# Splitting expert weights inside the feed-forward stage and parking them in DRAM, with smaller first batch and a limit on row transfers

## The reference

```python
# layer 0: attention with 16 heads, one k/v head and a computed position bias, then a spiking network
c = layernorm(attention(x))                       # 16 heads of 64
y = square(relu(c @ Wfc.T)) @ Wproj.T             # 256 -> 1024 -> 256
for 5 steps: mem = 0.9*mem + y - (mem > 1); count += (mem_new > 1)
x = x + count / 5
# layer 1: attention with a bias from a side input, then a transformer block with experts
X = layernorm(attention(x, fside))
X = X + mha(rmsnorm(X, g1))                       # 4 heads, one k/v head
xf = rmsnorm(X, g2)
top2 of xf @ Wr.T + bias, softmax weights         # 8 experts
moe = shared(xf) + sum over top2 of weight * expert(xf)   # each: silu(x W1) * (x W3) @ W2, 256 wide
x = x + X + moe
```

## Time and profile before

| | |
|---|---|
| median of 3 runs | 1442.61 us (1438.27 to 1443.07) |
| the profiled execution | 1443.43 us, its span 1441.7 us |
| PE busy | 1307.1 us (91%) |
| DVE busy | 1037.4 us (72%) |
| ACT busy | 897.6 us (62%) |
| POOL busy | 708.2 us (49%) |

### The profile page before, as it was taken

The page is one execution under the profiler, slowest core; times in us unless marked ns, Lnnn a source line. Parts: engine busy times, 40 slices in busy tenths (PEclk is TensorE's granted clock), DMA queues, the critical chain, the costliest instruction groups (busy, mean ns, idle before and its releaser), DMA issues.

```text
span 1441.7 us, 42824 instructions
## 1 busy us (share of the span) xinstructions
PE 1307.1 (91%) x15311; PEld 1157.7 (80%) x15312; DVE 1037.4 (72%) x2148; ACT 897.6 (62%) x2309; POOL 708.2 (49%) x797
## 2 busy tenths in 40 slices
PE   4899999999689999889999999689999789999980
PEld 3799999998579999778888888668788678888870
DVE  4798988988736465687887887768987686555446
ACT  3677777777356666656666666478775354555545
POOL 2556555564435454545445444357777562333330
PEclk8899999999799999999999999899997999999995
DMA  8200000001030000000000000020012623333319
GB/s 230 54 8 10 8 9 9 8 11 37 3 87 1 1 0 1 3 9 10 8 9 9 9 9 12 23 56 16 16 29 72 211 80 111 105 104 101 101 44 349
DMA packets 87025, 71.19 MB, mean 49 GB/s; under 512 B 49981, under 2 KB 80831, under 8 KB 85824
## 3 DMA queue, kind: packets, MB, share of 16 engines
q1 hardware_dynamic: 80320, 51.73, 12.7%
q0 software_dynamic: 6528, 17.05, 3.3%
HBM read 39.47 MB, written 24.02 MB: 44 GB/s over the span
## 4 chain that ended last, share of the span: by engine, by line
PE 56%; issue 20%; POOL 10%; DVE 9%; ACT 3%; DMA 1%; another core or an unknown queue 0%; ACTq 0%; POOLq 0%; DVEq 0%; SPq 0%
PE psQ L2348 9%; PE psQ L1957 7%; PE psW L2035 7%; PE psW L2327 5%; POOL pn L759 5%; PE psQ L2148 3%; POOL rq L785 3%; PE psS L2148 3%; PE psW L2136 3%; PE psM L2136 3%; PE psS L2059 2%; PE psT L1986 2%; PE psT L2070 2%; PE psM L2009 2%; PE psT L2316 2%
## 5 line engine op out<-in xcount | busy, mean ns | idle before, releaser
L1957 PE MATMUL psQ<-xT,wq 128*128 128x256 f32 x1536 | 224.8, 298 | 3.5 <-ACT cur L1117 1.8
L2035 PE MATMUL psW<-wout,oT 128*128 128x256 f32 x1536 | 207.8, 294 | 1.1 <-ACT oT L980 1.1
L1957 PEld LDWEIGHTS psQ<-xT,wq 128*128 128x128 f32 x1536 | 205.0, 201 | 4.4 <-issue 2.6
L2035 PEld LDWEIGHTS psW<-wout,oT 128*128 128x128 f32 x1536 | 196.6, 199 | 1.3 <-ACT oT L980 1.3
L2348 PE MATMUL psQ<-W,exT 128*128 (+1 forms) x624 | 172.3, 412 | 0.0
L759 POOL TENSOR_TENSOR pn<-ex,rden 128x1024 f32<-128x1024 f32 x64 | 124.5, 1945 | 45.2 <-DVE rden L1440 45.2
L980 ACT ACTIVATE oT<-psT,small 128x512 fp32r<-128x512 f32 x128 | 81.1, 684 | 91.3 <-PE psT L2070 91.2
L915 POOL DMA_INDIRECT results<-result,idx x72 | 70.1, 974 | 135.3 <-ACT result L1244 131.9
L803 POOL TENSOR_TENSOR hT<-hf,hT 128x512 fp32r<-128x512 f32 x64 | 85.8, 1341 | 102.1 <-ACT hT L1113 102.0
L771 POOL TENSOR_TENSOR masked_bias<-bias_t,negmask 128x1024 f32<-128x1024 f32 x32 | 68.8, 2150 | 132.6 <-DVE ex L1408 132.6
L1367 DVE SCALAR_TENSOR_TENSOR oT<-psT,small,oT 128x512 fp32r<-128x512 f32 x128 | 90.2, 746 | 58.3 <-ACT oT L980 58.3
(11 more groups left out here) (302 smaller groups left out, 3391.6 us busy)
## 6 DMA issues: line engine op xcount, KB each, us to landing
rows<-sorted SPq DMA_DIRECT2D x72, 132.0 KB, 2.1
both<-results SPq DMA_DIRECT2D x8, 1024.0 KB, 13.7
raw_w<-W SPq DMA_DIRECT2D x27, 256.0 KB
vv<-vp SPq DMA_DIRECT2D x256, 16.0 KB, 1.8
out<-X SPq DMA_DIRECT2D x8, 512.0 KB, 8.8
X<-x SPq DMA_DIRECT2D x1, 3584.0 KB, 18.1
bvv<-v_all SPq DMA_DIRECT2D x128, 16.0 KB
sorted<-rows SPq DMA_DIRECT2D x9, 132.0 KB
```

The lines of the kernel that those rows point to most:

```text
L1957: mm = nc.tensor.matmul(psQ[:, cc, h * QT:h * QT + QT], wq[w][:, k, c * P:c * P + P], xT[g % 2][u][:, k, :], start=(k == 0 and j == 0), st ...
L2035: mm = nc.tensor.matmul(psW[:, 0:D], oT[u][:, c, :], wout[w][:, c, :], start=(u == 0 and c == 0 and w == 0), stop=(u == 1 and c == CH - 1))
```

## The change

The split of all 27 pieces moves from the end of the block into the feed-forward network. After each of its first seven groups DVE alone splits 3 or 4 pieces (`PARKED`), high part and low part, in three buffers. SP loads raw pieces into the buffers, stores each split piece (512 KB) to a DRAM tensor `parked`, waits until it has landed, and loads the next raw piece into the same buffer. Later one DMA of 1536 KB loads an expert's finished weights, in place of three of 256 KB and the splits. SP waits for the first expert's weights before it issues the second's and the block's copies. DVE's loop over groups is written out.

The first batch of choices has 8 tiles instead of 12, and its choice is spread over four steps of the block; the second batch has 16, and its rank and places move to steps 1 and 2 of the shared expert. Each send waits until the send two before it has landed (two semaphores), in place of the wait for the shared expert's step; 16 of the sends stand in the block instead of 14.

```diff
-BATCHES = ((0, 12), (12, 24), (24, TILES))
-FIRST_CHOICE, SECOND_CHOICE, PLACES = (-14, -2, 5), (-13, -1, 6), (-11, 1, 8)
-RANKED_BEFORE, RANK = (19, 31), 7
-SEND_STEP, SENT_IN_BLOCK = 26, 14
+BATCHES = ((0, 8), (8, 24), (24, TILES))
+FIRST_CHOICE, SECOND_CHOICE, PLACES = ((-18, -17), (-2, -2), (5, 5)), ((-16, -15), (-1, -1), (6, 6)), ((-12, -11), (2, 2), (8, 8))
+RANKED_BEFORE, RANK = 17, {2: 1, 7: 2}
+SEND_STEP, SENT_IN_BLOCK, IN_FLIGHT = 26, 16, 2
...
-SPLIT_STEP = [-4, -3, -2, 0, 1, 2, 3, 4, 5] + list(range(10, 28))
+PARKED = [3] + [4] * (GROUPS - 2)
+PIECES = KD + 1
...
+        piece = [nc.alloc_sbuf_tensor_at(f"piece{i}", [P, 2, 2 * D], F32R, offset=pieces_at[i // 2] + 4 * K * (i % 2)) for i in range(3)]
...
+            def load_piece(n):
+                p, part = divmod(n, PIECES)
+                raw = raw_piece[n % 3][:, 1, :]
+                got = sem(f"p_raw{n % 3}")
+                if part < KD:
+                    for j, w in enumerate(("W1", "W3")):
+                        sp.dma_start(raw[:, j * D:j * D + D], a[w][p, part * P:part * P + P, :]).then_inc(got, 16)
+                else:
+                    sp.dma_start(raw.rearrange("p (k n) -> p k n", k=KD), a["W2"][p].rearrange("(k p) n -> p k n", p=P)).then_inc(got, 16)
+            def park(n):
+                p, part = divmod(n, PIECES)
+                sp.wait_ge(sem("p_lo"), n + 1)
+                sp.dma_start(parked[p, :, :, part * 2 * D:part * 2 * D + 2 * D], piece[n % 3][:].bitcast(F32)).then_inc(sem("p_kept"), 16)
+                sp.wait_ge(sem("p_kept"), 16 * (n + 1))
...
+            for n in range(3):
+                load_piece(n)
+            for n in range(PIECES * EP):
+                park(n)
+                if n + 3 < PIECES * EP:
+                    load_piece(n + 3)
             spread_v(LAYERS[1], load_block)
             def load_expert(p, slot, done):
...
+                sp.dma_start(W[:, slot, :, :].bitcast(F32), parked[p]).then_inc(done, 16)
             sp.wait_ge(sem("t_oev"), 2 * TILES)
-            for p in range(2):
-                load_expert(p, SHARED_SLOT + p, sem("e_first"))
+            load_expert(0, SHARED_SLOT, sem("e_weights"))
+            sp.wait_ge(sem("e_weights"), 16)
+            load_expert(1, SHARED_SLOT + 1, sem("e_weights"))
...
-            for p in (3, EP - 1, EP - 2):
-                load_expert(p, (p + 1) % EP, sem("e_rest"))
-            for p in range(4, EP - 2):
-                load_expert(p, p + 1, sem("e_last"))
+            for p in range(3, EP):
+                load_expert(p, (p + 1) % EP, sem("e_weights"))
...
-                if n >= SENT_IN_BLOCK and k == 0:
-                    pool.wait_ge(sem("e_xTp"), (t - SENT_IN_BLOCK // TOP_K) * 8 // 7 + 1)
+                reach(pool, sem(f"x_sent{n % IN_FLIGHT}"), 16 * (n // IN_FLIGHT))
                 send(t, k)
...
+            act.wait_ge(sem("p_kept"), 16 * PIECES * EP)
             for t in range(2):
                 norm_hi(TILES, t)
...
+            def split_piece(n):
+                part = n % PIECES
+                hi, lo = piece[n % 3][:, 0, :], piece[n % 3][:, 1, :]
+                raw = raw_piece[n % 3][:, 1, :]
+                dve.wait_ge(sem(f"p_raw{n % 3}"), (0 if n % 3 else 16) + sum(16 if m % PIECES == KD else 32 for m in range(n % 3, n + 1, 3)))
+                if part < KD:
+                    then(nc.vector.tensor_scalar(hi, raw, g2col[:, part:part + 1], None, ALU.mult))
+                    ins = nc.vector.scalar_tensor_tensor(lo, raw, g2col[:, part:part + 1], hi.bitcast(F32), ALU.mult, ALU.subtract)
+                else:
+                    then(nc.vector.tensor_copy(hi, raw))
+                    ins = nc.vector.tensor_tensor(lo, raw, hi.bitcast(F32), ALU.subtract)
+                ins.then_inc(sem("p_lo"), 1)
...
-            ffn(0, 0, first=True)
-            dve.wait_ge(sem("t_oev"), TILES)
-            ffn(1, 1)
-            with dve.Fori(1, GROUPS // 2 - 1) as pair:
-                ffn(2 * pair, 0)
-                ffn(2 * pair + 1, 1)
-            ffn(GROUPS - 2, 0)
-            ffn(GROUPS - 1, 1, last=True)
+            for g in range(GROUPS):
+                ffn(g, g % 2, first=g == 0, last=g == GROUPS - 1)
+                if g < GROUPS - 1:
+                    for n in range(sum(PARKED[:g]), sum(PARKED[:g + 1])):
+                        split_piece(n)
+                if g == 0:
+                    dve.wait_ge(sem("t_oev"), TILES)
...
-                    pe.wait_ge(sem("e_wlo"), 3 * EP if t else 3)
+                    pe.wait_ge(sem("e_weights"), 16 * EP if t else 16)
```

More of the change, by code:

```diff
@@ L336, in build @@
         count = sb("ffn_work", "count", [P, G4 * D], BF16)
+        pieces_at = (place["xT"][0] - 8 * K, place["ffn_work"][0])
+        piece = [nc.alloc_sbuf_tensor_at(f"piece{i}", [P, 2, 2 * D], F32R, offset=pieces_at[i // 2] + 4 * K * (i % 2)) for i in range(3)]
+        raw_piece = [nc.alloc_sbuf_tensor_at(f"raw_piece{i}", [P, 2, 2 * D], F32, offset=pieces_at[i // 2] + 4 * K * (i % 2)) for i in range(3)]
         place["ffn_work"][0] += 8 * K
@@ L662, in _ @@
             sp.wait_ge(sem("blanked"), 16 * (E + 1))
-            sp.wait_ge(sem("x_sent"), 16 * TOP_K * TILES)
+            for n in range(IN_FLIGHT):
+                sp.wait_ge(sem(f"x_sent{n}"), 16 * TOP_K * TILES // IN_FLIGHT)
             for r in range(ROUTED):
@@ L1208, in _ @@
             act.wait_ge(sem("t_oev"), 2 * TILES)
[L1210 to L1225, removed]
             def expert_step(i, m, shared=None):
@@ L1249, in expert_step @@
                     nc.scalar.activation(ehT[0][:], psT[:, 0, 0:D].rearrange("p (k q) -> p k q", q=P), ACT.Copy).then_inc(sem("e_hhi"), 1)
[L1251 to L1254, removed]
             def merged(i):
@@ L1617, in ffn, with then @@
                             split_q_lo(LAYERS[1], k)
-            ffn_in_lo(0, 0)
-            ffn(0, 0, first=True)
-            dve.wait_ge(sem("t_oev"), TILES)
-            ffn(1, 1)
-            with dve.Fori(1, GROUPS // 2 - 1) as pair:
-                ffn(2 * pair, 0)
-                ffn(2 * pair + 1, 1)
-            ffn(GROUPS - 2, 0)
-            ffn(GROUPS - 1, 1, last=True)
+            chained = 0
+            def then(ins):
+                nonlocal chained
+                chained += 1
+                ins.then_inc(sem("r_chain"), 1)
+                dve.wait_ge(sem("r_chain"), chained)
+            def split_piece(n):
[10 more added lines that the diff above has]
+                ins.then_inc(sem("p_lo"), 1)
+            ffn_in_lo(0, 0)
+            for g in range(GROUPS):
[5 more added lines that the diff above has]
+                    dve.wait_ge(sem("t_oev"), TILES)
             for t in range(2):
@@ L1719, in _ @@
             attention(LAYERS[1], lambda t: None, last_group)
[L1720 to L1740, removed]
             def logits_there(b):
@@ L1759, in every_tile, with choose @@
                 return v.unsqueeze(1).to_broadcast([P, high - low, E])
-            def choose(b, n):
+            def choose(b, n, part):
                 tiles = slice(*BATCHES[b])
@@ L1768, in choose @@
                 expert = xf_all[:, tiles, D + 1] if n == 0 else rc[0][:, tiles]
-                then(nc.vector.tensor_reduce(top_w[n][:, tiles], p, AX.X, ALU.max))
-                then(nc.vector.tensor_tensor(left, p, wide(top_w[n], b), ALU.is_lt))
-                then(nc.vector.scalar_tensor_tensor(left, left, float(E), index, ALU.mult, ALU.add))
+                if part == 0:
+                    then(nc.vector.tensor_reduce(top_w[n][:, tiles], p, AX.X, ALU.max))
+                    then(nc.vector.tensor_tensor(left, p, wide(top_w[n], b), ALU.is_lt))
+                    then(nc.vector.scalar_tensor_tensor(left, left, float(E), index, ALU.mult, ALU.add))
+                    return
                 then(nc.vector.tensor_reduce(expert, left, AX.X, ALU.min))
@@ L1804, in read_ranks, with places @@
                 dve.wait_ge(sem("r_read"), b + 1)
-            def places(b):
+            def places(b, k):
                 tiles = slice(*BATCHES[b])
-                if b == 2:
+                if b and k == 0:
                     read_ranks(b)
-                for k in range(TOP_K):
-                    mine = rt[1 + k][:, tiles, :]
-                    then(nc.vector.tensor_tensor(mine, mine, place_of[:, tiles, :], ALU.mult))
-                    then(nc.vector.tensor_reduce(pos[:, k, tiles], mine, AX.X, ALU.add))
+                mine = rt[1 + k][:, tiles, :]
+                then(nc.vector.tensor_tensor(mine, mine, place_of[:, tiles, :], ALU.mult))
+                then(nc.vector.tensor_reduce(pos[:, k, tiles], mine, AX.X, ALU.add))
+                if k == 0:
+                    return
                 nc.vector.tensor_copy(row_place[:, :, tiles], pos[:, :, tiles]).then_inc(sem("r_placed"), 1)
@@ L1885, in first_half @@
             def first_half(i):
-                if i in FIRST_CHOICE:
-                    logits_there(FIRST_CHOICE.index(i))
```

(22 more changed lines are left out.)

42 lines of the change are left out of this document (18 added, 24 removed).

## The result

The changed kernel takes 1469.11 us (median of 4 runs, 1467.8 to 1472.31); the kernel before took 1441.69 beside it. The ratio is 1.0198, 95% interval 1.018 to 1.0215: 27.4 us slower. The forecast was 13.6 us slower, 1456, with a range of 1436 to 1474.

A forecast was written before the change was run, and what follows sets the result against it. PE was taken to bound the kernel, busy for all 40 of 40 us in the feed-forward network. Losses of 27.6 us less 14 back gave +13.6: 1457.0 in the profile's terms, 1456 against the median, range 1436 to 1474.

The forecast's parts named there:

- How late DVE may be, and the fourth piece: Feed-forward network: DVE can lose about 5.65 us; a burst of 9.57 makes PE lose 3.9 in each of five groups.
- round trip of the fourth piece: Feed-forward bursts: store 4.5 us, load issue 0.47 and load 2.1 before the fourth piece can be split.
- the slack: Feed-forward network: DVE can lose about 5.65 us per group before PE's second `ffn_down` is held up.
- 0.7 per idle: Feed-forward network: clock PE loses after standing idle, taken between 0 and 1.4 us, five times, 3.5 in all.
- The 2 for the last group: Last feed-forward group: the burst exceeds DVE's idle by 2.9 us, delaying the next attention; 2 taken, bounds 0 and 4.7.
- 19.6 + 3.5 + 2: Feed-forward losses in us: PE's waits in bursts 1 to 5, lost clock, and the last group's delay.
- Start of the block: First expert's load delays the `bvv` copies about 4.8 us; loss taken as 2.5, between 0 and 4.8.
- Splits and choices in the block: Block's last steps: 3.5 us back from splits and waits removed, 2.5 from choosing 8 tiles instead of 12.
- At most 16.6 can come back ... I take half, 8: Shared steps: 102.1 us against 81.3 at the last step's length; stalls' cause left open, 8 us taken as returning.
- The added wait is at nothing: Sends: two in flight cost no wait if each lands within 2.56 us; a 132 KB row landed in 2.1.
- The rival of waiting sends: Shared stage: doubled weights space sends at 1.9 us, only 6 come back, +21.6, 1464 us; chance 0.12.
- 27.6 lost and 14 back: Whole kernel: feed-forward and block start lose 27.6 us; block's end and shared steps return 14, net +13.6.

The follow-up runs named there:

- the experiment with the late fourth piece: The changed kernel with the fourth piece of bursts 1 to 5 split after the next statistics instead of ahead of them: 1449.94 us, ratio 1.005.
- the limit alone: The kernel before with at most two sends in flight instead of the wait for the shared expert's steps: 1446.67 us, ratio 1.0037.
- without the parking: The changed kernel with splits and loads of the weights as before, keeping its batches, choices and two sends in flight: 1445.34 us, ratio 1.0032.
- four in flight: The changed kernel with four sends in flight instead of two: 1479.19 us, ratio 1.0248.
- both edits together: The changed kernel with the fourth piece split after the next statistics and four sends in flight: 1460.46 us, ratio 1.0128.

## Why the prediction was right and where it was wrong

**How late DVE may be, and the fourth piece: right.** The place (second `ffn_down` of groups 2 to 6), the cause (round trip of the fourth piece) and the slack held. The burst measured 8.0 us (451.34 to 459.37), predicted 9.57, and PE's five idles 2.13 to 2.36, predicted 3.9. The mis-sized term is the round trip: the store landed in 3.2 us where 4.5 was taken, the load in 2.2 for 2.1. The Trainium skill's fit ("DMA: Bandwidth & Descriptors", anatomy of one DMA), which it states for POOL's queue, had given 3.2 and 2.3 as estimates, and the trace agrees with it on these two. Clock was taken as 0.7 per idle and came to 1.3 in the mean (18.0 less 11.3 of idle, over five): none after the first idle, where the granted clock stayed at 1.00 (466 to 475), and more after the other four, where twelve matmuls took 2.93 us instead of 1.59 and the granted clock fell (0.70 from 490 to 495, a mean of its two levels, 1.2 and 2.4 GHz). The 2 for the last group came to nothing: its burst stands unchanged in the experiment with the late fourth piece, whose stage is as long as before. With 19.6 + 3.5 + 2 predicted and 18.0 measured, that experiment shows that the loss is the fourth piece and nothing else.

**Start of the block: wrong, without effect.** The copies were issued 18.0 us later than before (965.09 and 947.07), 0.5 beyond the shift of 17.5, where 4.8 was expected. The load and its wait held SP for 7.0 us (958.10 to 965.09), near the 7.5 taken, but they began 3.4 earlier against the shift. The 2.5 was too much.

**Splits and choices in the block: the sum came out by luck.** 3.5 + 2.5 were taken, 5.5 measured from the start of the attention to the first shared step (503.1 us instead of 508.6). But with the limit alone it is 506.2 (596.15 to 1102.30), without the parking 505.3 (595.82 to 1101.15), and with the fourth piece late, where the splits have left the block as well, 505.6 (595.23 to 1100.82). So 2.4 come with the limit, for which the sum had nothing here; at most 0.8 is left for the choices, and no run shows a part that is the splits'. Of the rest, 1.5 is that PE's first 24 matmuls of the attention took 3.10 us at a granted clock of 1.00 (616 to 620) instead of 4.61 at 0.66 (599 to 604).

**"At most 16.6 can come back ... I take half, 8": wrong in its cause.** 18.0 came back. The prediction left open what had made the stalls, and counted half of them among what comes back when the splits go. The limit of two alone brings the steps to 81.7 us with the splits in them, so the splits had been hidden; the stalls go with sends back to back. The prediction named sends as a possible cause under what would make it wrong.

**"The added wait is at nothing": the step that failed.** Its price was a row of 132 KB that SP loads in 2.1 us, less than two spacings. A send itself holds its place for about 3.2 us, and up to 8 under the weight loads, so the limit binds: 1.62 us each at best. That the sends end after the shared steps (28.61 us of idle on PE) is missing in the sum. The rival of waiting sends had the mechanism and 1464 us; it expected 1.9 us per send under loads, and that the first routed step starts no earlier than before; it started 22.8 later.

Net, the sum had 27.6 lost and 14 back; measured, in the spans, are 17.5 lost in the feed-forward network, 5.5 and 18.0 back, 28.8 lost ahead of the routed steps and 3.1 behind their start, where PE begins at a granted clock of 0.50 (1232 to 1237), the lower level of 1.2 GHz. The sign and the range held although a return of 18 was credited to the wrong part, at half its size, and a loss of 29 was left out: the two errors stand against each other, which is luck. Both come from one omission, what the limit on the sends does.

What makes the engines stall while POOL sends back to back isn't settled. Shown are that it goes with sends 1.28 us apart, and is gone at 1.62 (two in flight) and 2.46; that DMA carried 108 GB/s then, a quarter of what it did at 426 without a stall; that no packet of the instruction queues moved from 1180 to 1210; and that the profile names no engine of this core as the one that ended ACT's waits. Whether the pace or the number in flight does it, and which path the engines share with the sends, was not tried.

## What to carry to other kernels

Before work is put into the idle time of an engine, find the next thing that engine must deliver and how late that may be; a round trip inside a burst counts in full, and moving one piece behind the deadline was worth 19 us here. A limit on transfers in flight has two prices, its own pace and what it does to others, and they have to be read in different places: here it freed the shared steps of their stalls and made a new end of the stage out of the last send. Where a stage ends in two ways at once, a gain in one shows as a wait for the other.

## What was not expected of the hardware

During rows of indirect sends 1.28 us apart on POOL, PE, ACT and DVE stood idle for 10 us and more at a time (PE 10.93 with four in flight, 13.68 with both edits together), though DMA was far from full (108 GB/s). Beside the weight loads of 1.5 MB two sends took 6 to 8 us instead of 3.2, whether the loads were queued together or one by one. A store of 512 KB to DRAM landed in 3.2 us, sooner than the single load of that size before (4.5).
